# Two sorted expert stages: indexed transfers issued tile by tile behind TensorE's progress, the first scatter divided between two stages

## The chip, the core and the metric

One core of one Trainium2 chip. Its engines run their own instruction streams and wait for each other by semaphores: TensorE (PE; its weight loads are PEld), VectorE (DVE), ScalarE (ACT), GpSimd (POOL) and SyncE (SP, which only issues transfers here). The metric is the device time of one execution in microseconds (us), the median of several runs.

## What is computed

A chain of twelve steps on x, 2048 tokens of 128 channels in float32. The change touches the two steps `x + 0.5 * L1_ffn(layernorm(x))`, a mixture of 8 experts of which each token takes two:

```
def _L1_ffn_ref(x, rw1, rb1, rw2, rb2, we1, be1, we2, be2):     # D, E, H, K = 128, 8, 512, 2
    logits = silu(xt @ rw1 + rb1) @ rw2 + rb2
    _, idx = top_k(logits, K)
    w = softmax(where(mask, logits, -inf), axis=1)
    h = silu(einsum('nd,edh->enh', xt, we1) + be1[:, None, :])
    eo = einsum('enh,ehd->end', h, we2) + be2[:, None, :]
    return xt + einsum('ne,end->nd', w, eo)
...
    x = x + 0.5 * _L1_ffn_ref(_layernorm(x, axis=-1), ...)
    x = x + _L1_attn_ref(_layernorm(x, axis=-1), ...)
    x = x + 0.5 * _L1_ffn_ref(_layernorm(x, axis=-1), ...)
```

## The kernel before

`sorted_silu_ffn` computes such a step. The 2048 tokens are four blocks (n = 0 to 3) of 512. In each block the 1024 token-expert pairs are sorted by expert into 15 tiles (m = 0 to 14, `SLOT_TILES`) of 128 rows, so that each tile belongs to one expert. The program is written out by hand for each engine as a loop over n and m, and its order is the order of the code.

- **Sorting.** `dve_place` turns ranks (`pe_rank`, `prepare(n + 1, "rank")`) into a row number for each pair. `pool_scatter` (L496) writes the block's tokens into the DRAM tensor `slot_rows[n % 2]`: 8 indexed transfers (`indirect_dma_start`) of 64 KB, each of 128 rows of 512 bytes. SP reads the sorted rows back in four groups into `slots` (`bring_slots`, L1071; called at m = 10 for the next block, and it waits until all 8 transfers have landed), and TensorE transposes a group (`turn_slots`, L1162) at m = 12 (first group of the next block), 0, 4 and 8.
- **Experts.** For tile g = 15 n + m, SP brings the expert's weights (322 KB, L1063) into a ring of 6. TensorE runs `first_layer(g + 2)` (L1174, 4 matmuls, counted x8 in the trace) and then `second_layer(g)` (L1187, 4 matmuls, x8). ScalarE applies silu (`hidden_of`, L1274), VectorE adds the bias and takes the tile out (`out_y`, L1328), and SP writes groups of tiles to the DRAM tensor `y_rows[n % 2]` (`keep_y`, L1079).
- **Mixing.** `gather` (L1031) reads the results back in the order of the tokens: again 8 indexed transfers, into the one buffer `y_back`. It waits for the block's four groups in `y_rows`, and for `turn_y` of the block before it, which empties `y_back`. `mix` (L1038, L1040), `turn_y` (L1045) and `add_to_x` (L1051) of block n stand in block n + 2, at m = 4, 6 and 9.
- **The next blocks' routing** (layer norm L145, L161, L178; router L1146, L381, L390; tokens L484; rank L448, L450) lies between the tiles at the m given in the tables `prepare(...)`.
- **GpSimd's order.** It issues scatter 1, scatter 2, gather 0, scatter 3, gather 1, gather 2, gather 3, each of 8 transfers in a row. Scatter 0 is issued at the end of the stage in front (`Ahead.pool`): `top1_ffn` before the first of the two stages, `softmax_attention` before the second. In the second, gather 3 belongs to the stage behind it. A stage ends (`Block`) when all engines have finished in it.

## Time and profile before

| | us |
|---|---|
| median of 3 runs | 2883.95 (2881.16 to 2889.83) |
| the profiled execution | 2880.54 |
| its span (from the first to the last instruction) | 2878.7 |
| first of the two stages in the span | about 695 to 911 |
| second | about 1698 to 1911 |

Views used: the page's busy times; tables of busy time in chosen stretches of the span, with the clock granted to TensorE (PEclk, 1.00 is 2.4 GHz, 0.50 is 1.2 GHz), the mean busy share of the 16 DMA engines and what they moved; and the timeline, in which consecutive like instructions are merged into one row, with the idle time before it and what ended it in brackets. "issue" there is time in which the engine waited for nothing that the profile shows, "remote" a release whose source the profile does not name, PEq the sequencer. Lines L... are those of the kernel before.

### The profile page before, as it was taken

How to read it: one execution, taken by the hardware profiler on the slowest of the kernel's cores; microseconds unless marked ns; L12 is line 12 of the kernel's file. 1: busy time of each engine (PE TensorE's matmuls, PEld its weight loads, DVE VectorE, ACT ScalarE, POOL GpSimd, SP SyncE). 2: the span in 40 equal slices, each digit the busy share in tenths (PEclk: the TensorE clock that was granted, in tenths of full speed). 3: DMA queues.
4: the chain of work that ended last, by engine and by line, in shares of the span. 5: the costliest groups of instructions: out<-in, count | busy, mean ns of one | idle time of the engine just before them, and what ended most of it. 6: DMA issues, size and time to landing. Idle time of an engine off the chain costs nothing. (4 is left out here: it accounts for less than half of the span.)

```text
span 2878.7 us, 39791 instructions
## 1 busy us (share of the span) xinstructions
PE 2602.6 (90%) x13472; PEld 1296.0 (45%) x13472; DVE 1637.3 (57%) x2746; ACT 1264.0 (44%) x2914; POOL 531.3 (18%) x571
## 2 busy tenths in 40 slices
PE   7989999987786799999999977879999879999988
PEld 3446666654674222222222237754444544444433
DVE  5778888854223888888888511233342432333455
ACT  3652333333443488887887854431110231111243
POOL 1234666611325300000000013220000000000112
PEclk9988999998888699999999988889999889999999
DMA  2343232211562320110200026742220012120222
GB/s 96 99 144 111 89 98 91 73 40 63 154 169 74 79 39 15 22 32 3 40 14 3 4 74 194 212 133 81 66 88 34 26 60 89 59 89 30 60 45 60
DMA packets 132363, 212.55 MB, mean 74 GB/s; under 512 B 17969, under 2 KB 84273, under 8 KB 129425
## 3 DMA queue, kind: packets, MB, share of 16 engines
q1 hardware_dynamic: 128104, 202.08, 24.1%
q0 software_dynamic: 4096, 8.40, 0.9%
q8 instruction: 91, 1.49, 0.2%
q14 instruction: 72, 0.58, 0.1%
HBM read 177.22 MB, written 32.89 MB: 73 GB/s over the span
## 5 line engine op out<-in xcount | busy, mean ns | idle before, releaser
L2785 DVE TENSOR_REDUCE big<-psum 128x2 f32<-128x1024 f32 x512 | 603.7, 1220 | 76.9 <-PE psum L2582 73.0
L2739 ACT ACTIVATE probs<-psum 128x512 f32<-128x512 f32 x1024 | 553.3, 600 | 143.7 <-PE psum L2603 137.0
L2603 PE MATMUL psum<-big,k_ops 128*128 128x512 bf16 x1024 | 317.4, 386 | 9.3 <-ACT probs L2739 6.4
L1496 PE MATMUL psum<-big 128*128 128x512 f32 x512 | 232.9, 606 | 16.7 <-DVE big L1629 16.7
L2603 PEld LDWEIGHTS psum<-big,k_ops 128*128 128x128 bf16 x1024 | 81.1, 97 | 335.6 <-ACT probs L2739 261.7
L1521 PE MATMUL psum<-probs,big 128*128 128x512 f32 x512 | 222.0, 594 | 5.3 <-issue 3.6
L1510 PE MATMUL psum<-big 128*128 128x512 f32 x512 | 224.4, 594 | 0.0
L1274 ACT ACTIVATE hidden<-psum,big 128x128 f32<-128x128 f32 x480 | 135.7, 372 | 176.5 <-PE psum L1174 99.1
L1846 POOL TENSOR_TENSOR big<-big 128x512 f32<-128x512 f32 x32 | 40.4, 1267 | 908.4 <-ACT big L1811 867.3
L1328 DVE TENSOR_TENSOR probs<-psum,big 128x128 f32<-128x128 f32 x120 | 34.7, 290 | 277.2 <-PE psum L1187 172.2
L2582 PE MATMUL psum<-big,w_A_or_L_A 32*128 32x512 bf16 x1024 | 164.0, 397 | 18.6 <-DVE big L2785 14.4
L1174 PE MATMUL psum<-turned,big 128*128 128x128 f32 x960 | 147.1, 299 | 25.4 <-issue 17.3
L1187 PE MATMUL psum<-big,hidden 128*128 x960 | 145.4, 295 | 26.2 <-issue 13.9
L3558 POOL TENSOR_TENSOR big<-big 128x512 f32<-128x512 f32 x96 | 134.0, 1417 | 127.0 <-DVE big L3624 86.2
L1496 PEld LDWEIGHTS psum<-big 128*128 128x128 f32 x512 | 96.7, 194 | 132.8 <-issue 130.5
L1521 PEld LDWEIGHTS psum<-probs,big 128*128 128x128 f32 x512 | 96.5, 190 | 128.3 <-issue 125.4
L1187 PEld LDWEIGHTS psum<-big,hidden 128*128 128x128 f32 x960 | 131.2, 208 | 36.9 <-issue 36.8
L1174 PEld LDWEIGHTS psum<-turned,big 128*128 128x128 f32 x960 | 133.7, 214 | 30.9 <-issue 30.8
L1510 PEld LDWEIGHTS psum<-big 128*128 128x128 f32 x512 | 95.1, 190 | 116.5 <-issue 116.4
L2613 PE MATMUL psum<-probs,big 128*32 128x512 f32 x1024 | 138.3, 612 | 2.6 <-ACT probs L2739 2.6
L3618 DVE SCALAR_TENSOR_TENSOR big<-psum,big,probs 128x512 f32<-128x512 f32 x192 | 130.4, 740 | 11.5 <-PE psum L3338 10.4
L2613 PE MATMUL psum<-probs,xn 128*32 128x512 f32 x1024 | 136.8, 606 | 0.0
(465 smaller groups left out, 3723.0 us busy)
## 6 DMA issues: line engine op xcount, KB each, us to landing
big<-row_store SPq DMA_DIRECT2D x96, 512.0 KB
big<-in_experts SPq DMA_DIRECT2D x120, 322.0 KB
big<-step_rows SPq DMA_DIRECT2D x16, 1024.0 KB, 4.7
qkv_chunks<-big SPq DMA_DIRECT2D x48, 256.0 KB, 2.3
big<-qkv_chunks SPq DMA_DIRECT2D x16, 768.0 KB, 4.4
big<-since_rows SPq DMA_DIRECT2D x32, 256.0 KB, 5.3
big<-row_store SPq DMA_DIRECT2D x32, 256.0 KB, 5.1
slots<-slot_rows SPq DMA_DIRECT2D x24, 256.0 KB, 4.4
```

Source lines behind the costliest of these rows:

```text
L1174: mm = pe.matmul(k.bank[HIDDEN[g % 3]][:, c * P:(c + 1) * P], ring[g % RING][:, c * P:(c + 1) * P], turned[:, m, :], start=True, stop=True)
L1187: mm = pe.matmul(k.bank[6 + g % 2][:, 0:D], hidden[:, g % 3, c, :], w["we2"][:, bass.ds(expert * (C * D) + c * D, D)], start=(c == 0), sto ...
L1274: act.activation(hidden[:, g % 3, c, :], k.bank[HIDDEN[g % 3]][:, c * P:(c + 1) * P], ACT.Silu, bias=ring[g % RING][:, C * P + c:C * P + c ...
L1496: mm = pe.matmul(k.bank[4 + c % 2][:, :], w["gate"][:, e, c, :], scaled[:, e, :], start=(e == 0), stop=(e == E - 1))
L1510: mm = pe.matmul(k.bank[6 + c % 2][:, :], w["up"][:, e, c, :], scaled[:, E + e, :], start=(e == 0), stop=(e == E - 1))
L1521: mm = pe.matmul(k.bank[6 + e % 2][:, :], w["down"][:, e, c, :], inter[:, n % 2, c, :], start=(c == 0), stop=(c == C - 1))
L2582: mm = pe.matmul(k.row_pair[hp][:, (h % 2) * TB:(h % 2 + 1) * TB], row_q[g % 2][rows, at:at + P], row_k[g % 2][rows, kb * TB:(kb + 1) * TB ...
L2603: pe.matmul(k.bank[2 + m % 3][:, :], k_ops[:, g % 2, h, kt * P:(kt + 1) * P], q_ops[:, g % 2, i % QB, h, :], start=True, stop=True).then_i ...
L2613: mm = pe.matmul(k.bank[5][32 * h:32 * h + 32, :], v_group[g % 2][:, kt, h, :], probs[:, kt % 2, h, :], start=(kt == 0), stop=(kt == KT - 1))
L2739: act.activation(probs[:, kt % 2, h, :], k.bank[2 + m % 3][:, :], ACT.Exp, scale=SCALE).then_inc(expd.sem, 1)
L2785: dve.tensor_reduce(into, k.row_pair[hp].rearrange("p (h t) -> p h t", h=2), AX.X, ALU.max).then_inc(row_max.sem, 1)
L3558: pool.tensor_tensor(x_since[:, p, :, :], x, since[b][:, p, :, :], ALU.mult).then_inc(since_ready.sem, 1)
```

## The change

- `pool_scatter` and `gather` take a part of their 8 transfers; the waits at their head are made with the first.
- GpSimd's program in the stage is rewritten as a loop over n and m. Before each step m it waits (`reached`) until `first_layer` of tile m + 2 is done. In block n it issues scatter n + 1, one transfer at each m from 3 to 10, and gather n - 1, one at m = 2, 5, 8, 10, 11, 12 and the last two behind that. In the last block it issues gather 2 with one transfer a step from m = 0.
- `Ahead.pool(pool, scattered)`: in front of the first of the two stages only 3 of the 8 transfers of scatter 0 are issued, and the other 5 at the head of the stage. In front of the second all 8 stay where they were.
- Routing steps move one tile forward. On TensorE rank goes from m = 3 to 2, variance from 5 to 4, spread 8 to 7, hidden and tokens 10 to 9, logits 12 to 11, by_token 13 to 12; ScalarE and VectorE likewise. `dve_weigh` and `dve_place` go from behind `out_y` of m = 3 to before `out_y` of m = 2.

No instruction of TensorE, VectorE, ScalarE or SP is added or removed.

```
@@ class Dispatch
-    def pool_scatter(self, pool, n):
+    def pool_scatter(self, pool, n, first=0, end=2 * TPB):
         k, d = self.k, self.d
-        pool.wait_ge(self.placed.sem, self.placed.at(n))
-        pool.wait_ge(self.tokens_out.sem, self.tokens_out.at(n))
-        for i in range(2 * TPB):
+        if first == 0:
+            pool.wait_ge(self.placed.sem, self.placed.at(n))
+            pool.wait_ge(self.tokens_out.sem, self.tokens_out.at(n))
+        for i in range(first, end):
@@ class Ahead
-    def pool(self, pool):
+    def pool(self, pool, scattered=2 * TPB):
+        self.scattered = scattered
         if self.stage == "L1":
-            self.route.pool_scatter(pool, 0)
+            self.route.pool_scatter(pool, 0, 0, scattered)
@@ def top1_ffn
-                    ahead.pool(pool)
+                    ahead.pool(pool, scattered=3)
@@ def sorted_silu_ffn
-        def gather(pool, n):
-            for kept in y_kept:
-                pool.wait_ge(kept.sem, dma(kept, n + 1))
-            pool.wait_ge(y_turned.sem, y_turned.at(n - 1))
-            for i in range(2 * TPB):
+        def gather(pool, n, first=0, end=2 * TPB):
+            if first == 0:
+                for kept in y_kept:
+                    pool.wait_ge(kept.sem, dma(kept, n + 1))
+                pool.wait_ge(y_turned.sem, y_turned.at(n - 1))
+            for i in range(first, end):
...
-            def scatter(n):
-                if n > 1:
+            def scatter(n, first, end):
+                if n > 1 and first == 0:
                     for here in slots_here:
                         pool.wait_ge(here.sem, dma(here, n - 1))
-                route.pool_scatter(pool, n)
-
-            scatter(1)
-            for n in range(NB - 1):
-                if n + 2 < NB:
-                    scatter(n + 2)
-                gather(pool, n)
+                route.pool_scatter(pool, n, first, end)
+
+            def reached(n, m):
+                pool.wait_ge(pre.sem, pre.at(n * TILES + m + AHEAD))
+
+            if begun.scattered < 2 * TPB:
+                route.pool_scatter(pool, 0, begun.scattered)
+            for n in range(NB):
+                scattered, gathered = (0 if n + 1 < NB else 2 * TPB), (0 if n > 0 else 2 * TPB)
+                for m in range(TILES - AHEAD):
+                    if m > 0:
+                        reached(n, m)
+                    if m > 2 and scattered < 2 * TPB:
+                        scatter(n + 1, scattered, scattered + 1)
+                        scattered += 1
+                    if (n + 1 == NB or m % 3 == 2 or m > 9) and gathered < 2 * TPB:
+                        gather(pool, n - 1, gathered, gathered + 1)
+                        gathered += 1
+                if gathered < 2 * TPB:
+                    gather(pool, n - 1, gathered, 2 * TPB)
             if not leave:
                 gather(pool, NB - 1)
...
-                        prepare(n + 2, {1: "centre", 5: "variance", 8: "spread", 10: "hidden", 12: "logits", 13: "by_token"}.get(m))
+                        prepare(n + 2, {1: "centre", 4: "variance", 7: "spread", 9: "hidden", 11: "logits", 12: "by_token"}.get(m))
...
+                    if m == 2 and n + 1 < NB:
+                        route.dve_weigh(dve, n + 1)
+                        route.dve_place(dve, n + 1)
                     out_y(g)
```

GpSimd's rows before, from the end of `top1_ffn` (its last transfers are the first row here) through the first of the two stages; `slot_rows_0` and `_1` are the two scatter targets, `probs<-y_rows_0` and `_1` gathers:

```order
L817 UNCONDITIONAL_BRANCH
L496 DMA slot_rows_0<-desk_tokens,desk_row 1920x128 x8
L800 UNCONDITIONAL_BRANCH
L1113 UNCONDITIONAL_BRANCH
L496 DMA slot_rows_1<-desk_tokens,desk_row 1920x128 x8
L496 DMA slot_rows_0<-desk_tokens,desk_row 1920x128 x8
L1031 DMA probs<-y_rows_0,desk_row 128x128 x8
L496 DMA slot_rows_1<-desk_tokens,desk_row 1920x128 x8
L1031 DMA probs<-y_rows_1,desk_row 128x128 x8
```

The same place on GpSimd in the changed kernel, up to the scatter of block 3:

```order
L497 DMA slot_rows_0<-desk_tokens,desk_row 1920x128 x5
L497 DMA slot_rows_1<-desk_tokens,desk_row 1920x128 x8
L1034 DMA probs<-y_rows_0,desk_row 128x128
L497 DMA slot_rows_0<-desk_tokens,desk_row 1920x128 x3
L1034 DMA probs<-y_rows_0,desk_row 128x128
L497 DMA slot_rows_0<-desk_tokens,desk_row 1920x128 x3
L1034 DMA probs<-y_rows_0,desk_row 128x128
L497 DMA slot_rows_0<-desk_tokens,desk_row 1920x128 x2
L1034 DMA probs<-y_rows_0,desk_row 128x128 x5
L1034 DMA probs<-y_rows_1,desk_row 128x128
L497 DMA slot_rows_1<-desk_tokens,desk_row 1920x128 x3
L1034 DMA probs<-y_rows_1,desk_row 128x128
```

Gathers now stand between scatters, and the first transfer of gather 1 stands in front of all of scatter 3, which it stood behind before.

VectorE's rows before at the head of a block (L1328 is `out_y`, L442 `dve_weigh`, L459 to L479 `dve_place`):

```order
L1328 TENSOR_TENSOR probs<-psum,big 128x128
L1333 SCALAR_TENSOR_TENSOR x<-xn,x 128x512
L1328 TENSOR_TENSOR probs<-psum,big 128x128 x3
L442 TENSOR_SCALAR desk_share<-desk_half_tanh 128x4 x2
L459 TENSOR_TENSOR desk_over<-psum,w_const 128x32
```

The same place in the changed kernel (L1344 is `out_y` there):

```order
L1344 TENSOR_TENSOR probs<-psum,big 128x128
L1349 SCALAR_TENSOR_TENSOR x<-xn,x 128x512
L1344 TENSOR_TENSOR probs<-psum,big 128x128
L442 TENSOR_SCALAR desk_share<-desk_half_tanh 128x4 x2
L459 TENSOR_TENSOR desk_over<-psum,w_const 128x32
```

Two tiles fewer stand in front of the placing.

## Rows read from the trace of the kernel before

**Rows 1.** The page: busy time, share of the span, instructions, by engine.

```profile
PE 2602.6 (90%) x13472; PEld 1296.0 (45%) x13472; DVE 1637.3 (57%) x2746; ACT 1264.0 (44%) x2914; POOL 531.3 (18%) x571
```

**Rows 2.** Stretch, length, busy us (instructions) of PE, PEld, DVE, ACT, POOL; PEclk, DMA share, GB/s.

```profile
736.00:764.00 28.00, 25.71 (x222) 23.56 (x221) 8.09 (x39) 17.49 (x58) 0.25 (x1) 1.00 0.69 201
728.30:734.30 6.00, 2.57 (x21) 2.45 (x21) 1.44 (x3) 0.55 (x3) 2.98 (x4) 1.00 0.34 105
770.00:788.00 18.00, 7.50 (x27) 5.38 (x25) 1.36 (x4) 2.77 (x10) 10.46 (x11) 0.62 0.22 67
826.00:843.00 17.00, 7.96 (x29) 6.33 (x29) 1.38 (x4) 3.98 (x15) 9.20 (x10) 0.59 0.33 96
...
1731.90:1738.00 6.10, 2.28 (x16) 2.16 (x15) 1.44 (x3) 0.79 (x4) 3.08 (x4) 0.91 0.50 162
1777.00:1794.00 17.00, 7.12 (x25) 4.92 (x24) 1.05 (x3) 3.13 (x11) 10.14 (x11) 0.63 0.27 84
...
1750.00:1780.00 30.00, 28.13 (x227) 26.60 (x227) 8.65 (x39) 16.97 (x49) 7.51 (x8) 0.94 0.76 233
```

**Rows 3.** Timeline of GpSimd, start us, us: first and last of 16 transfers.

```profile
763.75 0.96 POOL L496 DMA_INDIRECT slot_rows<-desk_tokens,desk_row  x1 [31.56 <-DVE desk_row L479]
...
782.63 0.94 POOL L1031 DMA_INDIRECT probs<-y_rows,desk_row  x1 [0.30 <-issue]
```

**Rows 4.** Timeline of TensorE: two tiles outside, and parts of that burst.

```profile
754.31 1.05 PE L1187 MATMUL psum<-big,hidden 128*128 x8
...
756.09 1.06 PE L1187 MATMUL psum<-big,hidden 128*128 x8
...
772.98 0.27 PE L1187 MATMUL psum<-big,hidden 128*128 x1 [0.34 <-issue]
```

**Rows 5.** Timeline of ScalarE in that burst.

```profile
786.37 1.14 ACT L1274 ACTIVATE hidden<-psum,big 128x128 f32<-128x128 f32 x4 [12.95 <-remote]
```

**Rows 6.** Timeline of TensorE: the first group of blocks 1 and 2.

```profile
744.73 0.66 PE L1162 MATMUL psum<-w_const,slots 128*128 128x128 f32 x4 [1.93 <-DMA slots<-slot_rows]
...
798.03 0.91 PE L1162 MATMUL psum<-w_const,slots 128*128 128x128 f32 x4 [1.97 <-DMA slots<-slot_rows]
```

**Rows 7.** Timeline of TensorE: step m = 10 of block 0, its router work between.

```profile
736.45 1.13 PE L1174 MATMUL psum<-turned,big 128*128 128x128 f32 x8 [0.21 <-ACT turned L1268]
737.41 1.02 PE L1146 MATMUL psum<-xn,big 128*128 128x512 f32 x2
...
738.71 1.06 PE L1187 MATMUL psum<-big,hidden 128*128 x8
```

**Rows 8.** Timeline of SyncE: the sorted rows of block 1 and of block 3.

```profile
741.36 2.53 SPq L1071 DMA_DIRECT2D slots<-slot_rows  x4
...
843.92 2.03 SPq L1071 DMA_DIRECT2D slots<-slot_rows  x4
```

**Rows 9.** Timeline of GpSimd and TensorE: block 2.

```profile
817.71 1.33 POOL L496 DMA_INDIRECT slot_rows<-desk_tokens,desk_row  x1 [34.14 <-DVE desk_row L479]
...
819.00 0.66 PE L1045 MATMUL psum<-w_const,probs 128*128 128x128 f32 x4
```

**Rows 10.** Timelines where the first of the two stages begins: GpSimd, VectorE, TensorE, SyncE.

```profile
692.48 0.96 POOL L496 DMA_INDIRECT slot_rows<-desk_tokens,desk_row  x1 [0.30 <-issue]
...
686.72 0.69 DVE L973 SCALAR_TENSOR_TENSOR x<-psum,x 128x512 f32<-128x512 f32 x1 [0.82 <-PE psum L876]
...
695.38 2.04 PE L1146 MATMUL psum<-xn,big 128*128 128x512 f32 x2 [8.69 <-PEq L800]
...
703.92 1.11 PE L1162 MATMUL psum<-w_const,slots 128*128 128x128 f32 x4 [5.64 <-DMA slots<-slot_rows]
...
698.93 0.43 SPq L1071 DMA_DIRECT2D slots<-slot_rows  x1
```

**Rows 11.** Timelines at the end of the first stage: last gather transfer, and who waits.

```profile
904.75 0.94 POOL L1031 DMA_INDIRECT probs<-y_rows,desk_row  x1 [0.30 <-issue]
...
907.25 1.23 DVE L1038 TENSOR_TENSOR probs<-probs,desk_share 128x1024 f32<-128x1024 f32 x1 [6.66 <-DMA probs<-y_rows,desk_row]
```

More of the change, by code:

```diff
@@ L1208, in _ @@
                         first_layer(g + AHEAD)
-                    if m == 3 and n + 1 < NB:
+                    if m == 2 and n + 1 < NB:
                         prepare(n + 1, "rank")
                     if n + 2 < NB:
-                        prepare(n + 2, {1: "centre", 5: "variance", 8: "spread", 10: "hidden", 12: "logits", 13: "by_token"}.get(m))
-                        if m == 10:
+                        prepare(n + 2, {1: "centre", 4: "variance", 7: "spread", 9: "hidden", 11: "logits", 12: "by_token"}.get(m))
+                        if m == 9:
                             prepare(n + 2, "tokens")
@@ L1291, in _ @@
                         hidden_of(g + AHEAD)
-                    if m == 1 and n + 1 < NB:
+                    if m == 0 and n + 1 < NB:
                         prepare(n + 1, "second")
                     if n + 2 < NB:
-                        prepare(n + 2, {1: "centre", 5: "variance", 10: "hidden", 12: "logits"}.get(m))
-                        if m == 10:
+                        prepare(n + 2, {1: "centre", 4: "variance", 9: "hidden", 11: "logits"}.get(m))
+                        if m == 9:
                             prepare(n + 2, "tokens")
@@ L1343, in _ @@
                     g = n * TILES + m
+                    if m == 2 and n + 1 < NB:
+                        route.dve_weigh(dve, n + 1)
+                        route.dve_place(dve, n + 1)
                     out_y(g)
@@ L1346, in _ @@
                         add_input(n)
-                    elif m == 3 and n + 1 < NB:
-                        route.dve_weigh(dve, n + 1)
-                        route.dve_place(dve, n + 1)
                     if n + 2 < NB:
-                        prepare(n + 2, {6: "invert", 8: "norm", 13: "first", 14: "second"}.get(m))
+                        prepare(n + 2, {5: "invert", 7: "norm", 12: "first", 13: "second"}.get(m))
                     if n > 1:
```

## The prediction

> **What bounds the kernel now.** The page comes first: TensorE is busy 90% of the span [rows 1], so time can be won only where it waits or runs slowly. The busy times by stretch show where that is in the two expert stages. From 736 to 764, with GpSimd idle, TensorE ends 222 matmuls in 28.0 us at PEclk 1.00: 7.93 a microsecond [rows 2]. Of the stage's own work, a tile takes 1.78 us, from one second layer to the next [rows 4]. From 770 to 788 it ends 27 matmuls in 18.0 us, at 0.62; from 826 to 843, 29 in 17.0 us, at 0.59 [rows 2]. In both GpSimd issues indexed transfers back to back: in the first case 16 of them, from 763.75 to 783.57 [rows 3], one each 1.26 us (18.88 us over 15). The timeline shows what TensorE does meanwhile: single matmuls, each behind some 0.3 us or more of "issue", a time in which it waits for nothing that the profile knows [rows 4]. ScalarE stands 12.95 us behind a release without a source [rows 5]. It isn't the DMA engines' capacity: they are 0.22 busy at 67 GB/s there, and 0.69 at 201 GB/s in the good stretch [rows 2].
>
> So a burst of indexed transfers brings all engines nearly to a halt. It doesn't do so at once: the burst starts at 763.75, TensorE keeps its pace until about 770. Five transfers fit into those 6 us.
>
> The price of a burst is its length minus its matmuls at 7.93 a microsecond [rows 2]:
> - 16 transfers, block 1: 18.0 - 27/7.93 = 14.6 us; in the second stage 17.0 - 25/7.93 = 13.8.
> - 16 transfers, block 2: 17.0 - 29/7.93 = 13.3.
> - 8 transfers, block 0: 6.0 - 21/7.93 = 3.4; in the second stage 6.1 - 16/7.93 = 4.1.
>
> **The change part by part.**
>
> *Scatter 1, one transfer a tile (block 0).* A transfer now comes every 1.8 us or more instead of every 1.26, with room between. No stretch shows such a pace. From below, nothing is freed; from above all 3.4 + 4.1 us. I take all: the first five of every burst cost nothing even at full pace, and this pace is 30% lower. **-7.5 us.**
>
> *Scatter 2 and gather 0 (block 1).* 16 transfers of 1.26 us are 20.2 us of GpSimd, spread over m = 2 to 12, 11 tiles of 1.78 us and some 4 us of routing work: 23 to 24 us. At m = 5, 8 and 10 two are issued together. That is 85% of the burst's pace, hardly "spread". Bounds: nothing, or all 14.6 + 13.8 = 28.4 us. The nearest row is the head of a burst, where at full pace five transfers cost nothing, against single steps with two here; and if TensorE slows, the gate slows GpSimd too. I take 0.8 of it. **-22.8 us.** Bandwidth leaves room: 201 GB/s and 64 KB a tile of 1.78 us make 238 GB/s, and 233 were moved at 0.94 clock from 1750 to 1780 [rows 2].
>
> *Scatter 3 and gather 1 (block 2).* Here the order of the program matters. Gather 1 now leads, at m = 2, and waits until block 0's result has been turned out of the one buffer, which stands at m = 6: 819.00 to 819.66 [rows 9]. All of scatter 3 is queued behind it. When it is let go, the gates of m = 3 to 6 are long open and those up to 10 open faster than GpSimd issues: 12 transfers back to back (15 us), where 16 were, starting near 820 rather than at 817.71 [rows 9]. Only the last four are held by m = 11 and 12. Four transfers less are 5.0 us, at the burst's lost share of 13.3/17.0 = 0.78: 3.9 us a stage. Bounds: 0, or 8.8 (below). **-7.8 us.** Is scatter 3 late? Its last transfer is the 11th, at 820 + 10 x 1.26 = 832.6, and landed 2.5 us later (as the last gather transfer, 904.75 to 907.25 [rows 11]), at 835.1. SyncE asks for the sorted rows at 843.92 [rows 8], held by the tiles themselves: 8.8 us of cover.
>
> *Gather 2 and 3.* Gather 2 waits for the turn at m = 6 of block 3, as before; its gates are open by then. A burst of 8 stays, and so does gather 3. **0.**
>
> *The last scatter transfer at m = 10.* In block 0 the step m = 10 starts at 736.45; its first layer ends at 737.4, so the transfer is issued near 737.7 and has landed at 740.2. SyncE's read-back went at 741.36 [rows 7, 8], of which 1.3 us (737.41 to 738.71) is routing work that now lies a tile earlier: without it 740.1, measured from m = 10. They meet, and TensorE, which waits 1.93 and 1.97 us for these rows already [rows 6], waits a little longer. Bounds: 0, and 1.3, all the routing that no longer covers it. I take 0.5 at the four boundaries where the scatter is spread; behind block 2 it is covered. **+2.0 us.**
>
> *Scatter 0 in two parts.* The stage in front ends with GpSimd, at 693.44; VectorE's last work ends at 687.41 [rows 10]. With three transfers GpSimd ends near 687.1 and VectorE is last. TensorE's first matmul follows 1.9 us behind the end, so 6.0 us earlier, at 689.3. But it needs the sorted rows: five transfers from 689.3 on, the last at 694.4, landed at 696.9, two microseconds before SyncE's 698.93, where the weights no longer stand ahead of it. Of the 6.0 us some 1.9 remain (bounds 0 and 5). **-1.9 us.** In front of the second stage nothing changes.
>
> *Routing a tile earlier, placing before `out_y` of m = 2.* The same instructions. The placing delays one `out_y` by its chain of small operations, some 2.6 us; `second_layer` needs it two tiles (3.6 us) later. **0**, and a few tenths if that cover is gone. The 5 waits that split one transfer from the next stand only on GpSimd, and nothing but transfers is queued behind them.
>
> Sum: -7.5 - 22.8 - 7.8 + 2.0 - 1.9 = **-38.0 us**. The profiled execution took 2880.54 us, 3.4 less than the median, 2883.95; 38 off the median makes **2846 us**.
>
> **A rule that speaks against it.** In block 1 ScalarE, TensorE and VectorE all slow down while only transfers run [rows 2, 4, 5]. The Trainium skill, page "SBUF — State Buffer", section "Who interferes with whom", says that DMA never contends with a compute engine and that PE and ACT never wait on anyone. By that rule the burst would not be the cause and spreading it would free nothing. The trace of before disagrees in each of the five bursts measured, so this rule gets a small chance, as rival C.
>
> **The rivals.**
> - **A, the forecast** (0.50): 2846.
> - **B, the dense block stays half stalled** (0.23). At 85% of the burst's pace for 24 us, whatever fills up in 6 us fills later. Block 1 gives 0.3 of 28.4 us, block 2 nothing: -7.5 - 8.5 + 2.0 - 1.9 = -15.9, 2868. For it: the doubles at m = 5, 8 and 10, and stalls that deepen within a burst. Against: the gates hold GpSimd when TensorE slows.
> - **C, the change doesn't do what it says** (0.08): the halt hangs on the number of transfers or on something beside them, not on their pace. +2.0 - 1.9 = 0: 2884.
> - **D, slower** (0.07): as C, and the last scatter transfer at m = 10 becomes the wait. If its landing comes so late that the whole read-back (741.36 to 744.73, 3.4 us [rows 6, 8]) is exposed on top of today's wait, and TensorE then runs at 1.2 GHz for a while (2 us, an estimate: PEclk 0.62 and 0.59 in the stalled stretches [rows 2] show that the lower level follows such idling), four boundaries cost 4 x 5.4 = 21.6: with -1.9, 2904. It decides once a scatter lands later than about 3.4 us behind its gate and the bursts give nothing back. Against it: 2.5 us to land [rows 11].
> - **E, everything is freed** (0.12): the 28.4 us in full, and block 2 down to its sorted rows, which can be asked for at 835.1 instead of 843.92, 8.8 us a stage. -7.5 - 28.4 - 17.6 + 2.0 - 1.9 = -53.4: 2831.
>
> **How the numbers follow.** The likeliest case gives 2846. The range leaves out C and D (0.15) and the far end of E: from 2822, for E with its own error, to 2878, for B with half of its gain missing. A measurement can tell about 0.3%, 8.7 us, from no change: faster than 2875 are A, E and nearly all of B, 0.82; within, C and B's end, 0.11; slower D, 0.07.
>
> **What would show it.** Right: stretches of block 0 and 1 at PEclk 1.00 and near 7.9 matmuls a microsecond, no single matmuls behind "issue" before block 2; blocks 0 and 1 (first group to first group: 53.3 us from 744.73 to 798.03 [rows 6]) near 42 us; in block 2 a first indexed transfer released by TensorE's turn, then some 12 in a row, and a stall behind the sixth; TensorE's wait for the sorted rows at 2 to 3 us; the first stage starting 6 us earlier but its first group only 2. B would show as single matmuls from m = 7 on in block 1. Wrong would be a wait of TensorE for sorted rows of 5 us or more at the end of blocks 0 to 2, a wait for expert weights, or a halt behind five transfers at any pace.

## The result, and the profile after

| | us, median (runs) |
|---|---|
| kernel before | 2882.55 (2879.43 to 2889.83, 4) |
| changed kernel | 2819.49 (2817.51 to 2823.5, 4) |
| ratio | 0.9776, 95% interval 0.9762 to 0.9791 |
| span of the changed kernel's profile | 2817.2, before 2878.7 |

The gain is 63 us. The forecast was 38 and a range of 2822 to 2878, so the direction was right and the size too small. The experiments show something larger: the kernel before is slowed on some chips and not on others, and only where it is slowed does the change gain.

The page of the changed kernel, as in [rows 1]; TensorE's instructions are the same (89 matmul records are missing from this page). Its busy time is 40 us lower, but the missing records are part of that: between the two stages, where the code is the same, it falls from 733.1 us (4231 records, 911 to 1676) to 720.5 (4156 records, 885 to 1651). Some 22 us of it lie in the two stages:

```profile
PE 2562.3 (91%) x13383; PEld 1278.7 (45%) x13472; DVE 1636.1 (58%) x2746; ACT 1263.9 (45%) x2914; POOL 531.3 (19%) x571
```

The timeline of TensorE, the first group of sorted rows of blocks 0 to 3 of the first stage, as in [rows 6] (L1178 is L1162 of before, L1190 and L1203 the first and second layer, L497 the scatter, L1034 the gather):

```profile
701.92 1.11 PE L1178 MATMUL psum<-w_const,slots 128*128 128x128 f32 x4 [8.13 <-DMA slots<-slot_rows]
...
739.75 0.66 PE L1178 MATMUL psum<-w_const,slots 128*128 128x128 f32 x4 [2.41 <-DMA slots<-slot_rows]
...
777.63 1.11 PE L1178 MATMUL psum<-w_const,slots 128*128 128x128 f32 x4 [2.14 <-DMA slots<-slot_rows]
...
821.70 1.12 PE L1178 MATMUL psum<-w_const,slots 128*128 128x128 f32 x4 [4.10 <-DMA slots<-slot_rows]
```

The starts of these rows cut a stage into blocks. Before they were 703.92, 744.73, 798.03 and 847.78. Busy time by stretch for the same blocks, with the columns of [rows 2] (the last row lies inside block 2):

```profile
704.00:740.00 36.00, 33.56 (x273) 31.42 (x274) 10.08 (x42) 23.61 (x73) 7.66 (x8) 0.94 0.58 174
739.75:777.60 37.85, 34.69 (x298) 32.36 (x298) 10.71 (x45) 24.27 (x73) 14.47 (x15) 0.99 0.70 207
777.60:821.70 44.10, 36.23 (x271) 34.80 (x272) 11.56 (x46) 20.01 (x67) 15.18 (x16) 0.89 0.63 182
806.00:820.00 14.00, 7.99 (x47) 6.79 (x45) 1.68 (x5) 5.28 (x19) 8.76 (x10) 0.88 0.49 148
```

Block 1 runs at a clock of 0.99 with no stall, though GpSimd issues 15 of its transfers there. Its timeline shows how they are spaced (middle of block 1): one, two or three in a row, and then a pause of a microsecond until `first_layer` of the next tile.

```profile
758.86 0.96 POOL L497 DMA_INDIRECT slot_rows<-desk_tokens,desk_row  x1 [1.06 <-PE psum L1190]
760.12 0.97 POOL L1034 DMA_INDIRECT probs<-y_rows,desk_row  x1 [0.30 <-issue]
761.40 0.98 POOL L497 DMA_INDIRECT slot_rows<-desk_tokens,desk_row  x1 [0.30 <-issue]
763.52 0.96 POOL L497 DMA_INDIRECT slot_rows<-desk_tokens,desk_row  x1 [1.14 <-PE psum L1190]
```

Block 2 is as the prediction drew it. Gather 1 is released by the turn, transfers follow back to back, and TensorE stalls some 6 us behind the first. The timeline of GpSimd:

```profile
800.70 0.94 POOL L1034 DMA_INDIRECT probs<-y_rows,desk_row  x1 [22.10 <-PE psum L1048]
...
810.89 0.97 POOL L1034 DMA_INDIRECT probs<-y_rows,desk_row  x1 [0.30 <-issue]
813.90 0.97 POOL L497 DMA_INDIRECT slot_rows<-desk_tokens,desk_row  x1 [2.04 <-remote]
```

And that of TensorE:

```profile
807.77 1.13 PE L1190 MATMUL psum<-turned,big 128*128 128x128 f32 x8 [1.27 <-issue]
811.21 2.07 PE L1203 MATMUL psum<-big,hidden 128*128 x8 [2.31 <-DVE probs L1344]
```

There are nine in a row, not twelve: TensorE slows, the gate of the next tile closes, and the pause of 2.04 us ends the run.

### The profile page after: what moved, and what is told of

The parts are those of the page before. It is cut to its first block and busy times, and to the rows that moved or that the text cites. A ratio compares the mean times of both kernels' runs of the same rounds, so it can differ in the third digit from the quotient of the medians.

```text
span 2817.2 us, 39716 instructions
## 1 busy us (share of the span) xinstructions
PE 2562.3 (91%) x13383; PEld 1278.7 (45%) x13472; DVE 1636.1 (58%) x2746; ACT 1263.9 (45%) x2914; POOL 531.3 (19%) x571
## 5 line engine op out<-in xcount | busy, mean ns | idle before, releaser
L2619 PE MATMUL psum<-big,k_ops 128*128 128x512 bf16 x944 | 294.5, 386 | 13.3 <-ACT probs L2755 6.7
L1344 DVE TENSOR_TENSOR probs<-psum,big 128x128 f32<-128x128 f32 x120 | 34.8, 290 | 214.6 <-PE psum L1203 164.5
L1203 PE MATMUL psum<-big,hidden 128*128 x960 | 138.1, 290 | 9.1 <-DVE probs L1344 4.9
L1190 PE MATMUL psum<-turned,big 128*128 128x128 f32 x960 | 137.5, 290 | 9.3 <-issue 7.3
L1203 PEld LDWEIGHTS psum<-big,hidden 128*128 128x128 f32 x960 | 125.9, 204 | 17.2 <-issue 17.0
L1190 PEld LDWEIGHTS psum<-turned,big 128*128 128x128 f32 x960 | 126.5, 205 | 11.3 <-issue 11.1
```

Of the source, the lines that this page charges most:

```text
L1190: mm = pe.matmul(k.bank[HIDDEN[g % 3]][:, c * P:(c + 1) * P], ring[g % RING][:, c * P:(c + 1) * P], turned[:, m, :], start=True, stop=True)
L1203: mm = pe.matmul(k.bank[6 + g % 2][:, 0:D], hidden[:, g % 3, c, :], w["we2"][:, bass.ds(expert * (C * D) + c * D, D)], start=(c == 0), sto ...
L2619: pe.matmul(k.bank[2 + m % 3][:, :], k_ops[:, g % 2, h, kt * P:(kt + 1) * P], q_ops[:, g % 2, i % QB, h, :], start=True, stop=True).then_i ...
```

## The experiments

First all comparisons, since they only make sense together. Each was made on one chip, with the kernel before beside it. The chips carry numbers, except that of the first pair, which isn't recorded. A number in brackets is a count of runs or the 95% interval of a ratio.

| chip | kernel before | variant and ratio, or time of a single run |
|---|---|---|
| first pair | 2882.55 | the change 0.9776 |
| 12 | 2795.07 (29 runs) | e1 1.0039, e2 1.0006, e3 0.9984, e4 0.9999 |
| 12 | 2798.93 (12) | the change 1.0014 (0.9999 to 1.003); b2 2795.11, e5 2792.1, e6 2789.39 |
| 7 | 2795.57 (17) | e7 2795.86; e5b 0.9983 (0.9971 to 0.9995) |
| 8 | 2801.99 (1) | e8 2794.84 |
| 1 | 2886.17 (1) | e9 2845.91 |
| 14 | 2883.79 (7) | e10 0.9771 (0.9751 to 0.9792); e11 0.9841 (0.9824 to 0.9857) |
| 6 | 2794.34 (19) | e12 1.0013 (0.9998 to 1.0029); e13 1.0004 (0.9994 to 1.0015) |
| 6 | 2795.99 (13) | e14 0.9994 (0.9982 to 1.0006) |
| 12 | 2798.05 (13) | e15 0.9995 (0.9982 to 1.0009) |

The kernel before has two levels, 2794 to 2802 us on chips 6, 7, 8 and 12, and 2883 to 2886 on chips 1 and 14. The first pair was on the second kind. Below they are called quiet and halting chips. Chips 6 and 12 came back later at the same level. No halting chip came twice, so these are names for how a chip behaved when it was used: whether it always behaves so, or whether something beside this kernel made it, was not tested.

### One part at a time

e1, the new order and gates of GpSimd alone; in the changed kernel:

```
-                    ahead.pool(pool, scattered=3)
+                    ahead.pool(pool)
```
and the tables of `prepare`, `"rank"`, `"second"`, `dve_weigh` and `dve_place` back at their old m.

> One part of the change alone: GpSimd's new order with its gates (one transfer a tile, gather 1 ahead of scatter 3). The routing steps stay at the tiles they had before, and the first scatter is whole in the stage in front. Theory (what is freed is the halt of all engines behind some five indexed transfers in a row, and any pace that leaves gaps frees it): nearly the whole gain, 63 us, less the 4.2 that the first scatter gave and less 1 to 2 for a scatter that starts a tile later and has to catch up: 2882.5 - 57 = 2825, between 2820 and 2835; block 1 of both stages near 38 us, as in the changed kernel, with PEclk 1.00. Rival 1 (the routing a tile earlier is what frees the stages, since it lets the sorted rows come in time): 2860 to 2880 here, with block 1 still near 45 us or above. Rival 2 (a burst forms again, because placing stands a tile later and the gates are open by then): single matmuls behind issue in block 0 and 1, 2840 to 2860.

e2, in the kernel before only those tables and the placing moved:

> One part alone: the routing steps a tile earlier and the placing before the third tile's result is taken out; GpSimd keeps its order of before, 8 transfers in a row each. Theory: no effect on the halts, which only start a tile earlier: 2882.5 within 5 us, blocks 0, 1, 2 near 41, 53, 50 us. Rival 1 (routing carries a good part of the gain, above all of the 12.8 us in block 2 and the 7.8 in block 0): 2860 to 2870.

e3, in the kernel before only the first scatter divided:

```
-                    ahead.pool(pool)
+                    ahead.pool(pool, scattered=3)
...
+            if begun.scattered < 2 * TPB:
+                route.pool_scatter(pool, 0, begun.scattered)
             scatter(1)
```

> One part alone: the first scatter of the first stage divided, 3 transfers in front and 5 at the head of the stage; everything else as before. Theory: the time from the first scatter transfer to the first transposed group falls from 20.5 to about 16.3 us as in the changed kernel, and nothing else moves: 2882.5 - 4 = 2878.5. What the prediction said: 1.9 less, 2880.6. Rival (the five transfers at the head are followed at once by scatter 1, or delay something else): 2882 or more.

e4, the changed kernel with the turn made early:

```
-                    if (n + 1 == NB or m % 3 == 2 or m > 9) and gathered < 2 * TPB:
+                    if (n + 1 == NB or m in ((2, 5, 8) if n < 2 else (4, 6, 8)) or m > 9) and gathered < 2 * TPB:
...
-                    if m == 6 and n > 1:
+                    if m == (2 if n + 1 < NB or early else 6) and n > 1:
...
+                        soon = n + 1 < NB or early
-                        if m == 4:
+                        if m == (1 if soon else 4):
                             mix(dve, n - 2)
-                        elif m == 9:
+                        elif m == (5 if soon else 9):
```

> The changed kernel with the block before last mixed and turned earlier: mix at m = 1 instead of 4, its turn on TensorE at m = 2 instead of 6, the addition to x at m = 5 instead of 9 (in the last block of the second stage all three stay), and gather 1 in block 2 at m = 4, 6, 8, 10, 11, 12 and two behind. So gather 1 no longer waits in front of scatter 3, no 9 transfers come in a row, and gather 2 in the last block of the first stage is let go at m = 2, three or four at once and then one a tile. Theory (a run of transfers without gaps is what halts the engines): block 2 falls from 44.1 and 42.7 us to 39 or less in both stages, and some 2 us come off the last block of the first: 2819.5 - 4 to 13 = 2806 to 2815. Rival 1 (the 44 us of block 2 is not from the 9 in a row but from the number of transfers in a block, or from other work there): within 3 us of 2819.5. Rival 2 (mixing 2 us of VectorE at m = 1, next to the placing at m = 2, delays the results that the second layer waits for): 2820 to 2826.

These four fell on chip 12, a quiet one, while all four expectations had gone by 2882.5, and by a gain that wasn't there to be had. There e1 is 0.4% slower than the kernel before, e2 makes no difference, e3 is 4.7 us faster (from the first scatter transfer to the first group it took 16.19 us, the kernel before on this chip 21.25), and e4 makes none. So the question changed: where had the 88 us gone?

### The change and the kernel before once more

> The changed kernel once more, since the kernel before took 2795 us in the comparisons with the four variants and 2883 in the first comparison, and since in the profiles of those variants even 16 transfers in a row halt no engine. Theory (the halt behind a run of indexed transfers is there on some chips or at some times and not at others, and the change removes it only where it is there): one of two outcomes, told apart by the kernel before in the same comparison. If that takes about 2883: 2819, ratio 0.978. If it takes about 2795: the change has nothing to free, ratio between 1.000 and 1.005, 2795 to 2809. Rival (the first comparison was the odd one for another reason, and the change is worth its 2% everywhere): ratio 0.98 also beside 2795.

> The kernel before once more, for its profile beside that of the changed kernel in the same comparison. Theory: either 2883 us with blocks 1 and 2 of both stages at 50 to 55 us and single matmuls behind issue, or 2795 with those blocks at 36 to 40 and none. Nothing between: the whole difference of 88 us lies in the two stages behind runs of 5 or more indexed transfers, and the other parts differ by less than 10. Rival (the chips differ everywhere, by clock or memory): the 88 us spread over the whole span in proportion.

Ratio 1.0014: on a quiet chip the change is worth nothing. Busy time by stretch of the kernel before there, inside its run of 16 in block 1 (759.86 to 779.7) and inside that of block 2:

```profile
766.00:779.00 13.00, 10.51 (x88) 9.60 (x87) 1.76 (x5) 7.09 (x24) 9.76 (x11) 0.94 0.86 251
800.00:812.00 12.00, 11.13 (x95) 10.46 (x93) 2.35 (x7) 7.90 (x27) 9.05 (x10) 1.00 0.80 223
```

GpSimd issues at the same pace as in [rows 3], and TensorE ends 88 matmuls in 13 us and 95 in 12, 6.8 and 7.9 a microsecond, where [rows 2] had 27 in 18. Stretch by stretch, in us (from the marks above; the second stage likewise; "start" is from the first scatter transfer to the first group):

| | before, first pair | before, chip 12 | change, first pair | change, chip 12 |
|---|---|---|---|---|
| first stage: start | 20.51 | 21.25 | 16.32 | 16.34 |
| block 0 | 40.81 | 36.45 | 37.83 | 37.85 |
| block 1 | 53.30 | 36.85 | 37.88 | 40.06 |
| block 2 | 49.75 | 37.32 | 44.07 | 39.72 |
| block 3, to the stage's last turn | 61.61 | 56.06 | 63.22 | 57.08 |
| from there to the scatter of the second | 767.00 | 767.11 | 766.47 | 764.91 |
| second stage: start | 31.38 | 26.42 | 31.38 | 24.86 |
| block 0 | 42.08 | 36.87 | 37.26 | 36.94 |
| block 1 | 54.68 | 39.75 | 38.51 | 37.74 |
| block 2 | 49.77 | 38.48 | 42.69 | 38.38 |
| from there to the end of the span | 1024.40 | 1013.60 | 1015.97 | 1016.19 |

The 767 us between the stages are the same on both chips. Of the 85 us between the two profiles, 83 are in the two stages and their starts, where indexed transfers run in a row; most of the rest, 2.3 us, is behind the last turn. These numbers show no other difference of the chips. The changed kernel is still 20 us slower on the halting chip (2819.5 against 2800.2; 22.8 by the profiles), and of these some 6 stand in front of the second stage, where the eight transfers of scatter 0 are still issued in a row: 31.38 against 24.86 (24.9 to 27.0 in the profiles of quiet chips). Another 8.7 are block 2, and 6 lie behind it in the first stage.

On a quiet chip the change even has a price, which its other parts pay back. TensorE waits longer for the sorted rows of block 3, since scatter 3 is queued behind gather 1. The kernel before on chip 12, timeline of TensorE:

```profile
815.01 1.09 PE L1162 MATMUL psum<-w_const,slots 128*128 128x128 f32 x4 [3.88 <-DMA slots<-slot_rows]
```

The changed kernel there:

```profile
818.30 1.12 PE L1178 MATMUL psum<-w_const,slots 128*128 128x128 f32 x4 [6.54 <-DMA slots<-slot_rows]
```

And e4, where nothing is queued:

```profile
813.38 0.76 PE L1178 MATMUL psum<-w_const,slots 128*128 128x128 f32 x4 [3.55 <-DMA slots<-slot_rows]
```

### Is the halt only later on a quiet chip?

e7, in the kernel before each of scatter 1 to 3 followed by a copy of itself into tensors that nobody reads:

```
+        if n > 0:
+            for i in range(2 * TPB):
+                pool.indirect_dma_start(k.waste[k.wasted][:, :], bass.IndirectOffsetOnAxis(ap=d.row[:, n, i:i + 1], axis=0),
+                                        d.tokens[:, n % 2, i % TPB, :], None).then_inc(k.waste_sem[n % 2], 16)
```

> The suspected cost doubled on the kernel before: behind each of scatter 1, 2 and 3 of both stages GpSimd issues the same 8 transfers once more, into DRAM tensors that nobody reads. So the runs are 16 transfers in block 0, 24 in block 1 and 24 in block 2, the longest 30 us. Theory (where the halt is absent, it is absent at any length of a run): beside a kernel before of 2795, no single matmuls behind issue; only delays by order, since gather 0 and 1 come 10 us later: 2795 to 2805. Rival (the halt is everywhere and only begins later, behind more than 16 in a row): single matmuls from about the 17th transfer on in blocks 1 and 2, 5 to 8 us in each of four blocks: 2815 to 2830. Should the kernel before take 2883 here, each block has 8 transfers more in its halt: 6 x 10 x 0.78 = 47 us more, 2930.

2795.86 us beside 2795.57: 48 more transfers in runs of up to 24 cost nothing. On this chip the halt isn't there.

> The kernel before with every indexed transfer moving only the first 32 of 128 columns of a row (128 B in place of 512 B; the same number of transfers and rows, and so a quarter of the bytes). What is computed changes: the other columns of the sorted tokens and of the mixed results are not moved. Theory A (the issuing of the transfers, or their number of rows, is what halts the engines): where the kernel before takes 2883, this takes 2870 to 2885 too, with blocks 1 and 2 at 50 us. Theory B (the bytes that queue up): no halt, 2795 to 2810. Where the kernel before takes 2795, both give 2785 to 2797, and the run tells only the cost of the bytes.

This one also fell on a quiet chip and, as expected for that case, tells nothing on the halt. Its one run, 2789.39, lies inside the spread of the kernel before over all runs on that chip (2788.34 to 2803.88), so it doesn't tell what the bytes cost either. The question of the bytes was therefore built into the ladder.

### The ladder: how many in a row, and is it bytes?

```
+            ladder = [({3: 5, 8: 3}, {}), ({3: 4, 6: 4}, {9: 4, 12: 4}), ({3: 8}, {10: 8}), ({}, {3: 4, 6: 4})] if early else [
+                ({3: 6, 8: 2}, {}), ({3: 8}, {3: 8}), ({3: 4, 6: 4}, {9: 4, 12: 4}), ({}, {6: 4, 9: 4})]
```
(per block: scatter transfers at m, gather transfers at m; `early` is the first stage. The edit that shortens the rows of one block is not shown here.)

> A ladder of run lengths in one kernel, on the variant with the early turn, read block by block from its trace. First stage: block 0 five in a row, a pause, three; block 1 four, four, four, four; block 2 eight, a pause, eight; block 3 four and four. Second stage: block 0 six, a pause, two; block 1 sixteen in a row whose rows are a quarter as long (32 of 128 columns, so what is computed differs in that block); block 2 four times four; block 3 four and four. The kernel before takes about 2883 us on some chips and about 2795 on others, so there are two cases. Where it takes 2883 (theory: a halt begins 6 us behind the first of a run, whatever the bytes): no halt behind runs of four, none or under 0.5 us behind five and six, 3 to 4 us behind each run of eight, and still 13 us behind the sixteen short ones. Rival there (bytes that queue up): no halt behind the sixteen short ones. Second rival there (mean pace): halts also in the blocks with four times four. Where it takes 2795: no halt anywhere, 2787 to 2797, and the run says nothing of the ladder.

> The ladder of run lengths again, on whichever chip is given: its first run came where the kernel before takes 2802 us and shows no halt. The same two cases. Beside a kernel before of 2883: no halt behind four, none or under 0.5 us behind five and six, 3 to 4 us behind each eight, and 13 us behind the sixteen with a quarter of the bytes (theory: the issuing does it) or none there (rival: the bytes do it). Beside 2795: no halt anywhere, 2787 to 2797.

e8 was on chip 8 (quiet) and e9 on chip 1, which halts: the same kernel on both. Busy time by stretch of e9. First, six in a row from 1699.77, then its next 3 us; then sixteen short rows from 1745.19, before and after their sixth microsecond; last, four times four, some 2 us between:

```profile
1699.80:1706.00 6.20, 6.12 (x58) 5.68 (x57) 0.29 (x1) 4.57 (x8) 4.77 (x5) 1.00 0.87 268
1706.00:1709.00 3.00, 1.14 (x5) 0.60 (x4) 0.54 (x2) 1.32 (x6) 0.96 (x1) 0.94 0.43 144
1745.00:1751.00 6.00, 6.00 (x59) 5.65 (x58) 0.29 (x1) 4.57 (x8) 4.59 (x5) 1.00 0.77 240
1751.00:1767.00 16.00, 5.21 (x22) 4.45 (x21) 1.15 (x2) 1.14 (x4) 10.71 (x12) 0.67 0.29 83
...
765.00:785.00 20.00, 15.97 (x128) 14.36 (x127) 3.33 (x9) 10.46 (x37) 11.14 (x12) 0.97 0.74 215
```

And e8, inside the same sixteen short rows, on the quiet chip:

```profile
1721.00:1735.00 14.00, 13.08 (x115) 12.00 (x113) 2.35 (x7) 9.70 (x34) 10.65 (x12) 1.00 0.86 252
```

For 6 us TensorE is fully busy, at 240 and 268 GB/s; then it ends 22 matmuls in 16 us. TensorE's timeline of e9 there shows the pattern of [rows 4] again, one matmul each 1.4 us here:

```profile
1761.63 0.37 PE L1219 MATMUL psum<-big,hidden 128*128 x1 [0.75 <-issue]
1763.04 0.57 PE L1219 MATMUL psum<-big,hidden 128*128 x1 [1.04 <-issue]
1764.45 0.37 PE L1219 MATMUL psum<-big,hidden 128*128 x1 [0.85 <-issue]
```

Blocks, e9 less e8, in us: five and three 40.83 - 37.61 = 3.2; four times four 40.89 - 38.21 = 2.7; eight and eight 42.82 - 35.93 = 6.9; six and two 43.70 - 36.77 = 6.9; sixteen short 56.83 - 39.19 = 17.6; four times four in the second stage 41.08 - 38.95 = 2.1. What follows:
- The bytes are not the cause. A quarter of them halts the engines just as long (53.30 - 36.85 = 16.5 in the kernel before, 17.6 here). The number of transfers and of rows stayed the same, so which of these two it hangs on is open.
- The halt begins some 6 us behind the first transfer of a run, which is at the fifth or sixth.
- Six in a row cost far more than expected (6.9 us where under 0.5 was). That is more even than eight in a row cost in block 0 of the kernel before (40.81 - 36.45 = 4.4 and 42.08 - 36.87 = 5.2), so differences of 2 or 3 us between single profiles don't rank the lengths.
- Five cost 3.2 and four times four 2 to 3 us a block more than on a quiet chip. That is no more than the same block varies between quiet profiles (36.85 to 40.06 for block 1 in the table above), so this pair doesn't tell whether they cost anything. The next section does for the fours.

### Four in a row, and the pace alone, on a halting chip

e5, e5b and e10 are one kernel, e4 with

```
-                    if m > 2 and scattered < 2 * TPB:
-                        scatter(n + 1, scattered, scattered + 1)
...
+                    if m in (3, 6) and scattered < 2 * TPB:
+                        scatter(n + 1, scattered, scattered + 4)
+                        scattered += 4
+                    if m in ((3, 6) if n + 1 == NB else (9, 12)) and gathered < 2 * TPB:
+                        gather(pool, n - 1, gathered, gathered + 4)
+                        gathered += 4
```

> As the variant with the early turn, but GpSimd issues four transfers in a row at every third tile (scatter at m = 3 and 6, gather at m = 9 and 12, gather 2 at m = 3 and 6): as many a block as before, 95% of GpSimd's time in the middle of a block, but never more than four without a gap. Theory (where the halt is there, it begins behind the fifth of a run and a gap of a microsecond resets it): no halt in any block, blocks at 36 to 38 us, 2800 to 2812 where the kernel before takes 2883, and 2790 to 2797 where it takes 2795 (the scatter has landed three tiles earlier than with one a tile). Rival (what counts is the mean pace over some 10 us, not the run): where the halt is there, blocks 1 and 2 near 50 us and 2850 or more; where it isn't, no difference.

> The variant with four in a row at every third tile again, timed. Its one run took 2792.1 beside 2798.9 for the kernel before and 2800.2 for the changed one. Theory (without a halt to remove, a scatter spread to m = 10 lands late, the sorted rows of block 3 wait 6.5 to 7.6 us in place of 3.9 to 4.7, and four in a row by m = 6 end that, while the divided first scatter still gives its 4 us): ratio 0.997 to 0.999 beside a kernel before of 2795, that is 2787 to 2793. Where the kernel before takes 2883: 2800 to 2812. Rival (one run of luck): ratio 1.000 to 1.002.

> Four in a row at every third tile, timed on whichever chip is given; so far it stands at 0.998 beside a kernel before of 2795. The ladder showed beside 2886 that runs of four leave TensorE undisturbed, that from the fifth or sixth on it halts some 6 us behind the first, and that short rows halt it as much. Theory: beside a kernel before of 2883, blocks 0, 1 and 2 of both stages at 38 to 41 us and 2805 to 2815 (the changed kernel took 2819.5), ratio 0.973 to 0.977. Beside 2795: 0.997 to 0.999 again. Rival (fours at 95% of GpSimd's time halt at times, being near the edge): 2820 to 2835 beside 2883.

e11 is the kernel of e1.

> The new GpSimd order alone (routing at its old tiles, first scatter whole), timed on whichever chip is given; where nothing halts it took 1.0039 of the kernel before. Theory: the gain of the change comes from the pace, so beside a kernel before of 2883 nearly all of it is here: the changed kernel's 2819.5, plus 4 for the whole first scatter, plus the 7 us by which it stood behind the changed kernel's 2800 where nothing halts less those 4, so 2819.5 + 7 = 2826, between 2821 and 2833. Rival (the routing a tile earlier carries part of the gain): 2840 to 2870 beside 2883. Beside 2795: 2800 to 2810.

Both fell on chip 14, which halts. Fours reach 0.9771, the gain of the change. Each four is issued at GpSimd's full pace, and then it pauses until the third tile after; its timeline in block 1:

```profile
764.88 0.96 POOL L497 DMA_INDIRECT slot_rows<-desk_tokens,desk_row  x1 [2.02 <-PE psum L1190]
766.15 0.95 POOL L497 DMA_INDIRECT slot_rows<-desk_tokens,desk_row  x1 [0.31 <-issue]
767.41 0.96 POOL L497 DMA_INDIRECT slot_rows<-desk_tokens,desk_row  x1 [0.30 <-issue]
768.67 0.95 POOL L497 DMA_INDIRECT slot_rows<-desk_tokens,desk_row  x1 [0.30 <-issue]
771.80 0.97 POOL L1034 DMA_INDIRECT probs<-y_rows,desk_row  x1 [2.17 <-PE psum L1190]
```

That the length of a run counts, and not the mean pace of a block alone, is seen beside e9: six and two there were 8 transfers in 17.4 us and cost 6.9 us, sixteen in fours here take 24.5 us (758.13 to 782.60), a denser pace, and cost 2.4 to 4.8 us (41.57 less 39.21 in e5b or 36.79 in e5). On quiet chips the same kernel is at 0.9983, no more than the divided first scatter gave by itself (e3, 0.9984).

It missed its expectation of 2805 to 2815 by 5 us and stands at the edge of its rival's range, 2820 to 2835, in which fours halt at times. The blocks speak for a part of that rival. Blocks 0 to 2 took 40.25, 41.57 and 38.75 us where the same kernel had 37.15, 39.21 and 36.26 on a quiet chip. Over blocks 0 to 2 of both stages it is 240.9 us here against 225.2 in e5 and 228.8 in e5b: fours cost 2 to 3 us a block on this halting chip. The changed kernel, with no more than three in a row in blocks 0 and 1, took 151.5 us for these blocks of both stages together in the first pair and 152.6 on a quiet chip: no difference. In blocks 0 and 1 of the first stage of e10 the timeline of TensorE has no single matmuls behind "issue", and what takes the time there is open. Of the three versions timed on both kinds of chip (the change, the pace alone, the fours) this is the one at the front on both.

The pace alone (e11) reaches 0.9841: 45 of the 63 us, 6 less than the lower end of what was expected, and 2839.2 is next to the rival's 2840 to 2870, by which the earlier routing carries part of the gain. It is 20 us behind the changed kernel where the same two were 7 apart on chip 12 (2806.96 and 2800.17). So on a halting chip the earlier routing and the divided scatter are worth some 13 us more together, if the two halting chips can be compared. The timeline of GpSimd in its block 1 shows what a later placing does: scatter 2 starts late, the gates up to there are open, and five stand in a row.

```profile
761.54 0.98 POOL L497 DMA_INDIRECT slot_rows<-desk_tokens,desk_row  x1 [5.58 <-PE psum L1190]
...
766.63 0.97 POOL L497 DMA_INDIRECT slot_rows<-desk_tokens,desk_row  x1 [0.31 <-issue]
769.07 0.96 POOL L497 DMA_INDIRECT slot_rows<-desk_tokens,desk_row  x1 [1.46 <-remote]
```

Its block 1 took 41.81 and 43.10 us against 37.88 and 38.51, its start 20.77 against 16.32. That the five in a row are what takes the time in block 1 fits, and was not tested by itself.

> The changed kernel with the early turn (single transfers a tile in all blocks, none queued behind gather 1), timed again on whichever chip is given; where nothing halts it stood at 0.9999 of the kernel before. Theory: what is left of the halt in the changed kernel is block 2 (44.1 and 42.7 us, 9 in a row), and the run of 8 in the last block of the first stage, and both go: beside a kernel before of 2883, 2819.5 - 6 - 4 - 2 = 2807, between 2803 and 2812, ratio 0.974, with block 2 at 38 to 40 us. Rival (block 2 is held by something else there, as the 39.7 and 38.4 us on a chip without halts and the waits of 6.5 and 7.6 us for sorted rows suggest): 2815 to 2820. Beside 2795: 1.000 again.

> The routing steps a tile earlier, GpSimd's order as before, timed again; where nothing halts it stood at 1.0006. The pace alone brought 2839 beside 2884, the whole change 2819.5, so 20 us hang on the other two parts, of which the divided first scatter is worth 4. Theory (the earlier placing only gives the paced transfers room, so that no five stand in a row; by itself it moves the same runs a tile forward): beside 2883, within 5 us of it, blocks 1 and 2 at 50 to 55 us. Rival (the shift is worth its 16 us by itself): 2865 to 2870. Beside 2795: no difference, as before.

> The early turn with single transfers once more, since its last comparison came where the kernel before takes 2794 and nothing halts. Beside a kernel before of 2883: 2807, between 2803 and 2812, ratio 0.974, with block 2 at 38 to 40 us (theory: the run of nine is what is left), or 2815 to 2820 (rival). Beside 2795: 1.000 to 1.002, as the two times before.

> The same variant with the early turn and the same question, on another chip. Beside a kernel before of 2883: 2807, between 2803 and 2812, ratio 0.974, block 2 at 38 to 40 us (the run of nine is what is left), or 2815 to 2820 (something else holds block 2). Beside 2795: 0.999 to 1.002, as the three times before.

These four fell on quiet chips, 1.0013, 1.0004, 0.9994 and 0.9995. They confirm e4 and e2 there and say nothing of a halting chip. What the routing shift is worth by itself on one, and whether the early turn ends the 44 us of block 2, was not measured.

## Why the prediction was too small

By its own steps, in the first pair, in us:

| step | forecast | measured |
|---|---|---|
| block 0, both stages | -7.5 | -3.0 - 4.8 = -7.8 |
| block 1 | -22.8 | -15.4 - 16.2 = -31.6 |
| block 2 | -7.8 | -5.7 - 7.1 = -12.8 |
| last scatter at m = 10 (inside these blocks) | +2.0 | +1.8 |
| first scatter divided | -1.9 | -4.2 |
| gather 2 and 3 | 0 | block 3: +1.6 - 2.7 = -1.1 |
| all unchanged code | 0 | -4.1 |

- **Block 1 was mis-sized twice**, and is 9 of the 25 us: this is the largest step that failed, -22.8 forecast and -31.6 measured. The share of 0.8 was taken because the mean pace stayed at 85% of the burst's. But no run in block 1 is longer than three, and the whole halt went. The working had named the right row, the five free transfers at the head of a burst, and then set beside it a pace that no row supported. And the price of the halt, 28.4, was itself low. Length less matmuls at full rate counts only what was done inside the stall: against a chip without halts it is 16.5 + 14.9 = 31.4. That the rest is matmuls at 1.2 GHz around the stall and waits for results behind it is likely, and was not measured apart.
- **Block 2 was mis-sized.** The order was right, the first transfer released by the turn, the stall six microseconds behind. But twelve in a row were nine, since the gate holds GpSimd once TensorE slows and the run's own halt ends it. With the prediction's five free transfers and its lost share, (9 - 5) x 1.26 x 0.78 = 3.9 us of halt are left, and against the changed kernel on chip 12 there are 4.4 and 4.3. The prediction took off only the lost share of four transfers and never gave the five free ones to the run that stays.
- **The first scatter.** Its working held up to the request for the sorted rows. Measured from the first scatter transfer (683.41 before, 685.60 now), TensorE's first matmul came 6.5 us earlier where 6.0 were forecast, and SyncE's request went at 699.00, 13.4 us behind that transfer against 15.5: 2.1 us, where 1.9 were forecast. The other 2.1 is that the rows came 2.9 us behind the request instead of 5.0 (701.92 - 699.00, and 703.92 - 698.93). Three weight transfers had been issued 1.4 us ahead of it before (697.49), and 5.8 us now (693.17). The working had seen that they no longer stand in front and put no price on it; that they are the reason was not tested by itself.
- **The wait at m = 10** was right: 2.41, 2.14, 2.58 and 2.75 us against 1.93, 1.97, 2.07 and 2.15.
- **Unchanged code** ran 4.1 us faster in this pair. It is +2.2 up to the first scatter, -0.5 between the stages and -5.8 behind the last turn of the second (975.9 to 970.2). In the profiles of quiet chips the first of these stretches varies from 682.7 to 685.5, and the last took 973.7 us in the kernel before and 976.3 in the changed one, so this is taken as no effect of the change.
- **The rivals.** E, everything freed, was the nearest (2831) and still too small. It freed 3.2 us too little in block 1 and 4.8 too much in block 2, and the rest is the first scatter, the last blocks and the unchanged code. B was excluded by block 1. C, that the halt hangs on something beside the pace, was given 0.08 as a statement about this kernel. As one about chips it is half true: on four of the six numbered chips there is no halt, and on the one of them where the change was timed it made no difference. The rule of the Trainium skill that was weighed there, page "SBUF — State Buffer", section "Who interferes with whom", by which DMA never contends with a compute engine, agrees with the traces of the quiet chips. It doesn't account for those of the first pair and of chips 1 and 14, where the engines halt behind runs of transfers; by what they are held no trace names. The prediction treated one profile as the hardware, and no row of it could have shown this.

## What to carry to other kernels

When a profile shows all engines slowed with no releaser that it can name, look at the same kernel on a second chip before tuning against it: here 88 us of 2883 were there on some chips and not on others, and a change worth 2.2% on one was worth nothing on the next. Where indexed transfers must be issued, one to three in a row and then a pause of a microsecond left no halt that could be measured (blocks 0 and 1 of the changed kernel). Four in a row and then some 2 us kept the long halts away, still cost 2 to 3 us a block on a halting chip, and cost nothing on quiet ones, provided that what is waited for is issued first and that nothing that waits is put in front of it in the queue. Price a stall against the same stretch without it, not by counting what was done inside it.

## What was unexpected of the hardware

In the first pair and on chip 1, indexed transfers issued without a pause bring TensorE from 7.9 matmuls a microsecond to about 1.5 (27 in 18 us), from some 6 us behind the first transfer on, at a quarter of the bytes too (22 matmuls in 16 us, while the DMA engines moved 83 GB/s). On chip 14 the run of nine in block 2 of e11 does the same for a shorter time (16 matmuls from 812 to 818). On chips 6, 7, 8 and 12 sixteen in a row do nothing, and on chip 7 neither do 24, at the same issue pace of 1.26 us a transfer, and in the kernel before each stretch of code outside the two stages takes the same time to within 3 us. What differs between the chips, or at those times, is open. The traces of the two kinds show the same transfers, packets and bytes, and nothing in them names it.
